# Cross-attention and expert layer on one core: the next batch's shift prepared in tile 10, additions reordered, casts on ScalarE, row sums in two parts

## The reference, cut to what matters

```python
# x (8, 56, 128), ctx (8, 1500, 128), 16 heads of 64, all float32
xn = layernorm(x)
k, v = split(ctx @ Wkv); q = xn @ Wq
dots = einsum('bhnd,bhmd->bhnm', q, k) * 64**-0.5
dots = dots - (1.0 - mask)[:, None, :, None] * 1e6
attn = softmax(dots, axis=-1)                    # over the 1500 context rows
x = x + (einsum('bhnm,bhmd->bhnd', attn, v) merged) @ Wout + bout
t = layernorm(x)                                 # batch e goes to expert e, 8 experts
x = x + gelu(t[e] @ w1[e] + b1[e]) @ w2[e] + b2[e]
```

## Time and profile before

| | |
|---|---|
| median of 3 runs | 396.83 us |
| the profiled execution | 397.1 us, its span 395.3 us |
| TensorE busy | 386.4 us (98%) |
| VectorE busy | 298.4 us (75%) |
| ScalarE busy | 205.2 us (52%) |
| GpSimd busy | 56.7 us (14%) |
| granted TensorE clock | 1.0 in the profiled execution |

### The profile page before, as it was taken

The page is one execution under the profiler, slowest core; times in us unless marked ns, Lnnn a source line. Parts: engine busy times, 40 slices in busy tenths (PEclk is TensorE's granted clock), DMA queues, the critical chain, the costliest instruction groups (busy, mean ns, idle before and its releaser), DMA issues.

```text
span 395.3 us, 5513 instructions
## 1 busy us (share of the span) xinstructions
PE 386.4 (98%) x1701; PEld 278.5 (70%) x1701; DVE 298.4 (75%) x490; ACT 205.2 (52%) x273; POOL 56.7 (14%) x47
## 2 busy tenths in 40 slices
PE   7999999999999999999999999999999999999995
PEld 7766767767776876767676777667776776677674
DVE  4889678877887689877887689977887687266443
ACT  3546354475448345565456444675366354755421
POOL 0603400700070000700070001500060000000000
PEclk9999999999999999999999999999999999999999
DMA  7660020050005000033005000151001001200000
GB/s 257 203 210 26 2 78 1 4 152 1 2 0 147 10 2 2 14 120 133 0 7 148 0 0 0 32 163 72 0 24 54 0 0 28 84 2 0 3 2 3
DMA packets 20661, 19.62 MB, mean 50 GB/s; under 512 B 904, under 2 KB 17576, under 8 KB 20648
## 3 DMA queue, kind: packets, MB, share of 16 engines
q1 hardware_dynamic: 20648, 19.45, 15.8%
HBM read 19.21 MB, written 0.23 MB: 49 GB/s over the span
## 4 chain that ended last, share of the span: by engine, by line
PE 92%; DVE 4%; ACT 1%; DMA 1%; issue 1%; SPq 0%; DVEq 0%; ACTq 0%
PE ps_a L426 37%; PE ps_s L398 29%; PE ps_x L434 10%; PE ps_x L453 5%; PE ps_x L441 3%; PE ps_a L373 2%; PE ps_x L473 2%; PE ps_s L412 2%; PE ps_x L482 1%; DMA ex<-in_wk_t 1%; PE ps_x L412 1%; DVE chunk_max L764 1%; PE ps_x L346 1%; DVE ctxt_hi L781 1%; PE ps_s L366 0%
## 5 line engine op out<-in xcount | busy, mean ns | idle before, releaser
L426 PE MATMUL ps_a<-ex,ctx_sb 125*128 125x448 f32 x384 | 171.4, 541 | 0.0
L605 ACT ACTIVATE ex<-ps_s 125x896 f32<-125x896 f32 x96 | 88.1, 918 | 109.6 <-PE ps_s L398 83.4
L764 DVE TENSOR_REDUCE chunk_max<-ps_x 128x1 f32<-128x500 f32 x168 | 110.8, 675 | 30.8 <-PE ps_x L434 29.0
L426 PEld LDWEIGHTS ps_a<-ex,ctx_sb 125*128 125x128 f32 x384 | 71.3, 189 | 29.7 <-issue 23.9
L761 DVE TENSOR_TENSOR ex_sum<-ex_sum,ex 125x896 f32<-125x896 f32 x80 | 86.7, 1083 | 5.9 <-ACT ex L605 4.6
L434 PE MATMUL ps_x<-ctxt_hi,qk_hi 128*128 128x500 f32 x168 | 88.0, 526 | 1.7 <-DVE chunk_max L764 1.5
L398 PE MATMUL ps_s<-qk_hi,ctxt_hi 128*125 128x448 f32 x192 | 87.1, 534 | 0.0
L612 ACT COPY ps_s<-shift_row 125x896 f32<-125x896 f32 x80 | 72.9, 911 | 10.0 <-DVE shift_row L889 7.9
L398 PEld LDWEIGHTS ps_s<-qk_hi,ctxt_hi 128*125 128x125 f32 x192 | 35.9, 187 | 35.1 <-issue 35.0
L398 PE MATMUL ps_s<-qk_hi,ctxt_lo 128*125 128x448 f32 x192 | 57.3, 379 | 0.0
L398 PE MATMUL ps_s<-qk_lo,ctxt_hi 128*125 128x448 f32 x192 | 54.8, 367 | 0.0
(11 more groups left out here) (80 smaller groups left out, 257.0 us busy)
## 6 DMA issues: line engine op xcount, KB each, us to landing
ctxt_raw<-in_ctx_t SPq DMA_DIRECT2D x8, 750.0 KB, 7.1
ctx_sb<-in_ctx SPq DMA_DIRECT2D x8, 750.0 KB
w_sb<-in_w SPq DMA_DIRECT2D x4, 512.0 KB, 3.8
w_sb<-in_w SPq DMA_DIRECT2D x8, 256.0 KB, 4.3
ex<-in_wq_t SPq DMA_DIRECT2D x2, 256.0 KB, 3.7
ex<-in_wk_t SPq DMA_DIRECT2D x2, 256.0 KB, 4.5
att_n<-in_wv_t SPq DMA_DIRECT2D x1, 512.0 KB, 6.2
att_n<-in_w_out SPq DMA_DIRECT2D x1, 512.0 KB, 6.9
```

Of the source, the lines that this page charges most:

```text
L426: mm = nc.tensor.matmul(ps_a[:, c, 0:CH], ctx_sb[0:MT, u, t, :], ex[0:MT, t % RING, c * CH:(c + 1) * CH], start=(t == 0), stop=(t == TM - 1))
L605: nc.scalar.activation(half(ex[0:MT, slot, :]), src, ACT.Exp, scale=SCALE).then_inc(ex_ready, 1)
L764: nc.vector.tensor_reduce(chunk_max[:, k, t:t + 1], filled()[:, 0:MC], AX.X, ALU.max).then_inc(job_free, 1)
```

## The change

- Tiles 0 and 1 of batches 1 to 7 are seeded by ScalarE like the others. For that the next batch's shift is prepared in tile 10 of the batch ahead: the two shift jobs stand at (10, 2) instead of (0, 1), `shifts` at (10, 0) instead of (11, 1), the 21 maxima end at (9, 2) or (9, 0) instead of (10, 2). `shift_row` has two buffers. Batch 0 keeps its own old scheme.
- The additions are no longer made one per tile. 1 and 2 stand in tile 3, 3 at (5, 1), 4 at (7, 1), 5 at (9, 1), 6 at (10, 0), 7 at (10, 2), 8 and 9 at (11, 0), and 10 and 11 at (0, 0) of the next batch.
- The casts of `qk` and `ctxt_raw` move from VectorE to ScalarE.
- The row sums of batches 0 to 6 are made from a float32r high part (cast on ScalarE) and a low part (subtraction on VectorE), four float32r matmuls instead of two float32 ones.
- The loads of batch 1 are issued ahead of the first expert weights.

```diff
-    SHIFT_AT = (0, 1)
-    SEEDED = TM - 2
+    FIRST_SHIFT_AT, SHIFT_AT = (0, 1), (TM - 2, 2)
+    ADD_AT = {(3, 0): (1, 2), (5, 1): (3,), (7, 1): (4,), (9, 1): (5,), (10, 0): (6,), (10, 2): (7,), (11, 0): (8, 9)}
+    ADD_LATE = (10, 11)
...
@@ sync
             load_ctx(Batch(None, 0))
+            load_batch(Batch(None, 1))
             load_experts(0)
-            load_batch(Batch(None, 1))
@@ tensor
-                seed = t >= 2
+                seed = b.off > 0 or t >= 2
                 if seed:
-                    pe.wait_ge(seeded, b.at(SEEDED, t - 1))
-                else:
-                    wait(pe, ex_ready, b.at(TM, t - 1))
+                    pe.wait_ge(seeded, b.at(TM, t - 1))
...
+                        nc.tensor.matmul(bank[:, 0:CH], ones_r[0:MT, :], sum_hi[0:MT, cols], start=True, stop=False)
+                        mm = nc.tensor.matmul(bank[:, 0:CH], ones_r[0:MT, :], sum_lo[0:MT, cols], start=False, stop=True)
...
+                    if prepare and at == SHIFT_AT:
+                        pe.wait_ge(shift_ready, b.later(1).at(1, 1))
+                        shift_jobs()
@@ scalar
+            def sum_high_part(b):
+                act.wait_ge(ex_summed, b.at(TM - 1, TM - 1))
+                nc.scalar.copy(sum_hi[0:MT, :], ex_sum[0:MT, b.parity, :]).then_inc(sum_hi_ready, 1)
...
+                    if t == 0 and prepare and not first:
+                        qk_hi_part(b.later(1))
+                        ctxt_hi_chunk(b.later(1), 0)
...
                     if t + 2 < TM:
+                        if t == 0 and first:
+                            jobs.n += 2
+                            act.wait_ge(job_free, jobs.value())
                         seed(b, t + 2)
+                    elif prepare:
+                        if t + 2 == TM:
+                            jobs.n = FIRST_JOBS if first else jobs.n + 2
+                            act.wait_ge(job_free, jobs.value())
+                        seed(b.later(1), t + 2 - TM)
+                    if t == 0 and b.off > 0:
+                        sum_high_part(b.later(-1))
+                    if t < 2 and prepare:
+                        ctxt_hi_chunk(b.later(1), t + 1)
@@ vector
+            def shift_copies(b):
+                wait(dve, seeded, b.at(TM, -TM - 2))
+                for c in range(2):
+                    nc.vector.tensor_copy(shift_row[:, b.parity, c * CH:(c + 1) * CH], filled()[:, 0:CH]).then_inc(job_free, 1)
+            def sum_low_part(b):
+                dve.wait_ge(sum_hi_ready, b.at(1, 1))
+                nc.vector.tensor_tensor(sum_lo[0:MT, :], ex_sum[0:MT, b.parity, :], sum_hi[0:MT, :].bitcast(F32),
+                                        ALU.subtract).then_inc(sum_lo_ready, 1)
...
                 for t in range(TM):
                     drain((t, 0))
                     between((t, 0))
-                    if t > 1:
-                        add_tile(b, t - 1)
-                    elif t == 0 and b.off > 0:
-                        add_tile(b.later(-1), TM - 1)
+                    add((t, 0))
                     between((t, 1))
                     drain((t, 1))
+                    add((t, 1))
                     between((t, 2))
                     drain((t, 2))
                     between((t, 3))
+                    add((t, 2))
```

More of the change, by code:

```diff
@@ L484, in out_job, with shift_jobs @@
                 mm.then_inc(job_ready, 1)
+            def shift_jobs():
+                for c in range(2):
+                    shift_rows(job()[:, 0:CH], P, c, start=True).then_inc(job_ready, 1)
             def iteration(b, prepare=True, pair=None):
                 def jobs_at(at):
-                    if at == SHIFT_AT:
-                        for c in range(2):
-                            shift_rows(job()[:, 0:CH], P, c, start=True).then_inc(job_ready, 1)
+                    if b.off == 0 and at == FIRST_SHIFT_AT:
+                        shift_jobs()
+                    if prepare and at == SHIFT_AT:
+                        pe.wait_ge(shift_ready, b.later(1).at(1, 1))
+                        shift_jobs()
                     if b.off == 0 and at in FOLD_AT:
@@ L665, in iteration @@
             def iteration(b, prepare=True, pair=None):
+                first = b.i is None and b.off == 0
                 for t in range(TM):
-                    if t == 0:
-                        jobs.n += 2
+                    if t == 0 and prepare and not first:
+                        qk_hi_part(b.later(1))
+                        ctxt_hi_chunk(b.later(1), 0)
                     if t == SUM_AT[0] and b.off > 0:
@@ L672, in iteration @@
                         jobs.n += sum(at > SUM_AT for at in MAX_AT[b.parity]) if prepare else 0
-                        jobs.n += 4 if pair is not None else 0
+                        jobs.n += 3 if pair is not None else 0
                     if pair is not None:
@@ L684, in iteration @@
                     if t + 2 < TM:
+                        if t == 0 and first:
+                            jobs.n += 2
+                            act.wait_ge(job_free, jobs.value())
                         seed(b, t + 2)
+                    elif prepare:
[7 more added lines that the diff above has]
+                        ctxt_hi_chunk(b.later(1), t + 1)
+                jobs.n += 1 if pair is not None else 0
             def drain_fold(n):
@@ L882, in xn_transposed @@
                                       filled()[:, 0:(end - first) * P]).then_inc(job_free, 1)
+            def shift_copies(b):
+                wait(dve, seeded, b.at(TM, -TM - 2))
+                for c in range(2):
+                    nc.vector.tensor_copy(shift_row[:, b.parity, c * CH:(c + 1) * CH], filled()[:, 0:CH]).then_inc(job_free, 1)
[3 more added lines that the diff above has]
+                                        ALU.subtract).then_inc(sum_lo_ready, 1)
             def iteration(b, prepare=True, pair=None):
                 def drain(at):
-                    if at == SHIFT_AT:
-                        wait(dve, seeded, b.at(SEEDED, 0))
-                        for c in range(2):
-                            nc.vector.tensor_copy(shift_row[:, c * CH:(c + 1) * CH], filled()[:, 0:CH]).then_inc(job_free, 1)
+                    if b.off == 0 and at == FIRST_SHIFT_AT:
+                        shift_copies(b)
+                    if prepare and at == SHIFT_AT:
+                        shift_copies(b.later(1))
                     if b.off == 0 and at in FOLD_AT:
@@ L908, in between @@
                 def between(at):
-                    if prepare and at == QK_HI_AT:
-                        qk_hi_part(b.later(1))
-                    if prepare and at in CTXT_HI_AT:
-                        ctxt_hi_chunk(b.later(1), CTXT_HI_AT.index(at))
+                    if b.off > 0 and at == SUM_LO_AT:
+                        sum_low_part(b.later(-1))
                     if b.off > 0 and at == REFINE_AT:
@@ L922, in between, with add @@
                         gelu(pair)
-                    if prepare and at == (TM - 1, 1):
+                    if prepare and at == (TM - 2, 0):
                         shifts(b.later(1))
+                def add(at):
+                    if at == (0, 0) and b.off > 0:
+                        for n in ADD_LATE:
+                            add_tile(b.later(-1), n)
+                    if prepare:
+                        for n in ADD_AT.get(at, ()):
+                            add_tile(b, n)
+                    elif at[0] > 1 and at[1] == 0:
+                        add_tile(b, at[0] - 1)
                 for t in range(TM):
```

47 lines of the change are left out of this document (29 added, 18 removed), and 8 rows, old and new, of the table MAX_AT.

## The result

The changed kernel took 404.65 us, the median of 4 runs (401.47 to 407.96), beside 396.89 us of the kernel before (396.64 to 400.62). The ratio is 1.0153, with a 95% interval of 1.0106 to 1.0200: slower, clear of noise though by less than 2%. The ratio leaves out the longest execution (407.96 us, granted clock 0.973). On the 396.83 us of the front page that is 402.9 us (401.0 to 404.8). The forecast of 398.3 had the sign right and the size too small; 402.9 lies inside its range (392.5 to 403.5), the kernel's own median 1.2 us above it. The three executions that count have spans of 399.7, 402.3 and 403.4 us at mean granted clocks of 0.991, 0.983 and 0.983. The profiled execution took 404.09 us with a span of 402.3 us, where the one before had 397.1 and 395.3.

A forecast was written before the change was run, and what follows sets the result against it. The prediction took TensorE, busy without reserve, to bound the kernel: -5.6 - 5.0 + 11.1 + 0.6 + 0.4 = +1.5 us gave 398.3 us. Its own range was 396 to 403, the 8-in-10 range 392.5 to 403.5.

The forecast's parts named there:

- The savings: TensorE in batches 1 to 7: 5.6 us from 14 shift pairs, 5.0 us from row sums, together 10.6 us.
- ScalarE at nothing: Between tile 10 and tile 2: ScalarE's 5.3 us of added work per batch would cost nothing, covered by TensorE's tiles.
- Rival 3: Batch starts: casts dearer than estimated make ScalarE late, 0.8 us in six batches, 4.9 us, giving 403.2 us; chance 0.12.
- The price of a pair batch: End of batches 2, 4 and 6: TensorE stands still 3.7 us each for shift and gelu, 11.1 us in all.
- the walk: VectorE's new queue laid onto batch 4's timeline from the (9, 1) maximum, putting gelu's end at 246.5.
- its 242.6: Time in batch 4 when VectorE ends addition 6, gelu_cap and two shift copies, ahead of additions 7 to 9.
- Rival 1: Pair batches: VectorE's reserve keeps the out_job wait at 1 us or less, giving 390.2 us; chance 0.23.
- The start and end of batch 0: Batch 0: 0.4 us at the start for a maximum behind ScalarE's casts, 0.6 us at the end for the shift.
- rival 2: TensorE's clock falls to 1.2 GHz behind each of three pauses, 3 x 2.7 us more, giving 406.4 us; chance 0.08.
- the sum: Whole kernel: savings, pair-batch waits and batch 0's costs add up to +1.5 us, without any clock fall.
- the forecast's own signs of being wrong: gelu ending before TensorE reaches out_job, odd batches above 39.2 us, or granted clock under 1.0 past the first pause.
- dearer pauses: Upper end for a pair batch: 4.7 us, with 0.2 us more on each of five operations added ahead of gelu.

The follow-up runs named there:

- sums_alone: The kernel before with only the row sums made in two parts (four float32r matmuls); 392.97 us, ratio 0.9875.
- experiment 6: experiment 4 with additions spread over earlier tiles, 396.11 us; the same with the casts of qk and ctxt_raw back on VectorE, 403.43 us.
- spare_in_wait: The changed kernel with ten spare float32 matmuls ahead of out_job's wait for gelu in batches 2, 4 and 6; 398.30 us, ratio 1.0034.
- experiment 3: The changed kernel with additions 7, 8 and 9 moved behind gelu on VectorE; 399.74 us, ratio 1.0079.
- experiment 4: The changed kernel with gelu_cap ahead of shifts, ScalarE's sigmoid ahead of the seed and additions 6 to 9 behind gelu; 401.56 us, ratio 1.0113.
- experiment 5: experiment 4 with addition 5 also moved from (9, 1) to behind shifts at (10, 0); 406.07 us, ratio 1.0214.
- Experiment 8: experiment 4 with GpSimd's subtractions held back until the scores of tile 3 stand ready; 396.77 us, ratio 0.9966.

## Why the prediction came out as it did

**The savings.** Right. Batch 5 lasted 39.48 us, and its first tile was 0.74 us longer by the clock (2.32 from first scores to L427, 1.58 at full clock): 38.74, as forecast (38.7), 1.52 less than before. The row sums at L450 and L451 start at steps of 0.20 to 0.21 us, and `sums_alone` gives 4.7 us in the span and 5.0 by its ratio for the forecast's 5.0. Batch 1 was 0.35 us above. 0.26 of it lie in its tile 10 (3.42 us, 3.16 in batch 5), where the shift jobs start 0.13 us after `shift_diag` has ended and the two halves of tile 8's product are 1.44 us apart (1.17 in batch 5): a short wait for the shift, which the forecast had put at 0 in odd batches and the trace doesn't name. The other 0.09 stay open. The pair batches saved 1.35 to 1.40 us each, also a little under 1.52. In all the savings come to 9.8 us for 10.6.

**ScalarE at nothing.** Right. The trace after has the casts at 608 ns for a chunk (estimate 0.58) and about 0.94 us for 896 columns:

```profile
L631 ACT CAST ctxt_hi<-ctxt_raw 128x500 fp32r<-128x500 f32 x21 | 12.8, 608 | 0.0
L646 ACT CAST sum_hi<-ex_sum 125x896 fp32r<-125x896 f32 x7 | 6.6, 939 | 2.1 <-DVE ex_sum L806 2.1
L635 ACT CAST qk_hi<-qk 128x896 fp32r (+1 forms) x7 | 6.5, 935 | 0.0
```

TensorE waits once for them, 1.1 us at the start of batch 0. Rival 3 is out; in experiment 6, casts back on VectorE cost 6 to 8 us.

**The price of a pair batch.** Right in mechanism and nearly in size. From the start of the (9, 1) product to the end of `gelu` the walk gave 246.5 - 235.7 = 10.8 us (10.9 with its 242.6 put right to 242.7, 240.2 + 1.00 + 0.34 + 1.14); the trace has 237.25 to 248.05, 10.8. The waits at L492 are 2.88, 2.86 and 2.88, those for the shift 0.75, 0.56 and 0.59: 3.4 to 3.6 together, for 3.7. Taking the clock out (1.4, 0.9 and 1.4 of it fall inside), batches 2, 4 and 6 last 49.4, 49.2 and 49.2 us; the forecast said 49.4. Rival 1 fell with this: VectorE's reserve over a batch did nothing for the stretch behind (9, 1).

**The start and end of batch 0.** Forecast 0.4 + 0.6, measured 0.5. Batch 1 starts 0.9 us later than before, but 0.4 of that is the pair of shift jobs for batch 1, which now stands in batch 0; batch 7 has none and is shorter by as much. At the start the wait of 1.1 us for `ctxt_hi` was absorbed whole, since the scores of tile 3 start at 38.80, before at 38.90. At the end the shift's wait was 0.38. The earlier load of batch 1 was not run alone.

**What failed is the step from rival 2 to the sum.** I gave the clock 0.08 because no row before showed a pause of this kind, and put it beside the forecast instead of in it. It was not an alternative to the pauses but their consequence, three times out of three in the trace, and a granted clock under 1.0 past the first pause was one of the forecast's own signs of being wrong. It cost 5.8 us by the rows, and `spare_in_wait` gives 6.2 by the spans and 4.7 by the ratios; the rival's price of 3 x 2.7 was right for the first pause and too high for the other two. Savings of 9.8, pauses of 10.5, 0.5 in batch 0 and 5.8 for the clock add up to the 7.0 us by which the span grew; the forecast's own terms give +1.2 for its +1.5. That 402.9 still lies in the range is partly luck: the range left the clock out, its upper end was meant for dearer pauses (4.7 us each), which didn't come, and the clock cost less than rival 2's 8.1. The Trainium skill, "TensorE: Matmul & The Clock Gate", section "Why this matters for your kernels", says that idle gaps between bursts of matmuls put the clock back to half; by that rule the trace after agrees, at pauses of 2.9 us. Of the three pauses of 1.9 us in experiment 3, one did it too.

**Where the two later misses (experiments 4 and 5) came from** was not in the prediction: an addition priced by itself, put where another engine works. Experiment 8 gives the whole miss of experiment 4 to it; for experiment 5 no such run was made. The Trainium skill, "SBUF — State Buffer", section "Who interferes with whom", says that a VectorE instruction with two inputs in SBUF contends with a GpSimd instruction that reads SBUF. The runs agree: 2.04 us beside GpSimd, 1.09 at most without it.

## What to carry to other kernels

Where one engine is busy all the time, write out the queue of the engine that feeds it for the ten microseconds around the moved work; a reserve over a whole batch says nothing there. If the walk gives that engine a pause of some microseconds, put a colder clock behind it into the sum, not beside it. Work put off moves the wait to where it lands: check what it stands in front of, and which other engine runs beside it there. Holding that other engine back can just hand the stretch to a later instruction: compare the lengths of all tiles, not only of the one that was to be mended.

## What the hardware showed that I had not expected

- The clock fell behind all three pauses of 2.9 us and behind one of three of 1.9 us, and stayed at the lower level for 6.8, 3.4 and 3.4 us in the kernel after. Equal pauses had unequal prices (2.7, 1.6 and 1.5 us); the clock fell 0.9 us before, 0.6 us after and 0.3 us before the matmuls came back.
- An addition of 896 columns with both inputs in SBUF took up to 2.04 us in experiment 4 (2.13 in the kernel after) beside GpSimd's subtractions instead of 1.08, and GpSimd's own 448 columns 1.99 instead of 1.13. In the kernel before the additions didn't pay: all 80 stayed at 1.09 or less, and the subtraction that began beside one (245.53) took 1.82. The maxima, which read PSUM, kept their 0.68.
- Spare matmuls of no use made the changed kernel 5 to 6 us faster, by keeping the clock up through a pause that they did not shorten.
